# A twelve-part transformer step on one core: the dense network as one stage over chunks, and a retention that also norms and turns for the quantised network behind it

## The chip, the core and the metric

The kernel is one program on one core of a Trainium2 chip (eight cores, five engines each: PE or TensorE, DVE or VectorE, ACT or ScalarE, POOL or GpSimd, SP or SyncE). The metric is the device time of one execution in microseconds (us), lower is better; the time before is the median of 3 runs.

## What is computed

The input x has 128 rows of 32 positions with 128 channels, so 4096 tokens of 128 channels in float32. Twelve parts are added to it, each on a layer norm of the running x. Three are cross attentions over a context of 257 tokens, one is a linear transformer of six layers, three are mixtures of experts, and so on. Cut to what the change touches:

```python
x = x + _L2_attn_ref(_layernorm(x, axis=-1), ...)    # 8: retention
x = x + _L2_ffn_ref(_layernorm(x, axis=-1), L2_ffn_w1, L2_ffn_b1, L2_ffn_w2, L2_ffn_b2)   # 9: quantised network
...
x = x + _L3_attn_ref(_layernorm(x, axis=-1), ...)    # 11: its _block is below

def quant_act_uint8(x):
    s = jax.lax.stop_gradient(jnp.maximum(jnp.max(x), EPS)) / 255.0
    q = jnp.clip(jnp.round(x / s), 0.0, 255.0) * s
    return (_ste(x, q), s)

# inside _block of part 11, behind its attention
h2 = _layernorm(hs, ln2_g, ln2_b)
m = _student_linear(h2, *cf)        # 128 -> 512
m = _gelu_new(m)
m = _student_linear(m, *cm)         # 512 -> 128
return hs + m
```

The quantised network needs the largest value of its whole normed input before it can use any of it.

## The kernel before

`program` keeps the running x in SBUF as X, 32 tiles of 128 tokens by 128 channels, and runs the twelve parts one after the other. CHUNKS is 8 and TPC is 4: a chunk is four tiles, 512 tokens. A part is a `Scope` with tiles, semaphores and one block in which each engine has its own written-out list of instructions; engines meet only at semaphores. When a block closes, all engines meet, and POOL clears the scope's semaphores one after the other before the next block opens. `retention` has 33 semaphores and one for its weights, a `front` 15, `experts` 11.

**Retention** (part 8) is one pipeline over 32 tiles. Every engine runs `step(s)` for s from -16 to 41, and in a step each helper runs for the chunk whose place it is: `run(s, (4, squares))` runs `squares(c)` when s = 4c + 4. A tile's scores go from PE (`scores`, L965) to DVE (`decay`, L1116) and back to PE (`weighted`, L979). Each chunk is also normed by ACT (`apply`, L1052), turned by PE (`turn_normed`, L988), projected (L993, L1011, L1016), and afterwards centred and scaled by group (DVE L1125, L1129, L1134, L1140, ACT L1069, L1076, POOL L937), turned back (`turn_outputs`, L1022), gated (POOL L941), projected (`output`, L1029) and added to X (`add`, DVE L1145, place 9). The gate's Silu (ACT L1065) and the square root (ACT L1076) each have an ACT_TABLE_LOAD ahead of them in every chunk.

**The front of the quantised network** is a scope of its own, `front(core, "q_front", lambda n: None, hT_all)`. It works in pairs of chunks: DVE takes statistics of X (L207, L211), POOL makes the reciprocal root (L223, L225), DVE applies it (L233), PE turns the tiles (L1212), ACT copies them to `hT_all` (L1235), the transposed normed x of all 4096 tokens. `quantised_ffn` then fetches its weights with one DMA (SP, L151) and takes the maximum over hT_all on DVE (L2496).

**The dense network** of part 11 is two scopes: `front(core, "t_front", ...)` as above, here on the tile `inner` (written by the attention ahead of it, and the `hs` of the reference), and `experts(core, "t_mlp", source, hT_all, None, 1, 4, "gelu_tanh", base=inner, out_bias=True)`. `experts` is a hardware loop (`Fori`) over the eight chunks on each engine, here with one job of four blocks:

```python
last = pe.matmul(psum[:, (m % RING) * width + half], w("up")[...], rhs, ...)      # L1798, x4
act.wait_ge(s_base, c + 1)                                                        # before the first gelu
act.activation(hidden[:, j % 2, f], psum[:, at], ACT.Gelu_apprx_tanh, ...)        # L1851, x4
last = pe.matmul(psum[:, 4 + j % 2, ...], hidden[:, j % 2, f, ...], w("down")[...], ...)   # L1810, x16
dve.tensor_tensor(X[:, chunk], X[:, chunk], spread(w("bo"), TPC, 1), ALU.add)     # L1863
dve.tensor_tensor(X[:, chunk], X[:, chunk], base[:, chunk], ALU.add)              # L1866, counts s_base
dve.tensor_tensor(X[:, chunk], psum[:, 4 + j % 2]..., X[:, chunk], ALU.add)       # L1883
dve.wait_ge(s_acc, c * NJ + NJ)                                                   # end of the chunk
```

The order on PE is up(c), down(c), up(c+1), and so on. A float32 matmul is two records in the profile, so one chunk shows 8 of L1798 and 32 of L1810; a transposition of a tile is one record.

## Time and profile before

| what | us |
|---|---|
| median of 3 runs | 4488.55 |
| lowest and highest run | 4482.6, 4489.98 |
| the profiled execution, its own time | 4482.12 |
| its span | 4480.1 |
| mean granted TensorE clock, share of full speed | 0.893 |

The profile shows one execution. A row of the timeline has the start in us from the span's start, the time from the first start to the last end of the merged instructions, the engine, the line, the operation with output and inputs, the count, and in brackets the idle time of the engine just before and who ended it. PEld is the weight load of PE; PEq or ACTq is a sequencer. PEclk is the clock granted to TensorE as a share of 2.4 GHz, so 0.50 is 1.2 GHz.

### The profile page before, as it was taken

To read this page: it belongs to the slowest core of one execution; us is meant where nothing else is said; L and a number is where in the kernel's file an instruction comes from. 1 tells how busy PE (TensorE), PEld (TensorE's weight loads), DVE (VectorE), ACT (ScalarE), POOL (GpSimd) and SP (SyncE) were. 2 spreads that over 40 slices of the span, in tenths; PEclk is the share of its full clock that TensorE was granted. 3 is DMA by queue.
4 is the path that set the end of the run, shared out by engine and by line. 5 is a ranking of instruction groups with operands and counts; after the bars stand their busy time and mean duration, and the time that the engine had idled before them with its cause. 6 is when DMAs were issued, how large, how long until landed. Compare 5 with 4: busy or idle time off the path is not lost. (4 is left out here: it accounts for less than half of the span.)

```text
span 4480.1 us, 120532 instructions
## 1 busy us (share of the span) xinstructions
PE 3517.0 (79%) x44658; PEld 2454.9 (55%) x44662; DVE 2798.7 (62%) x7126; ACT 2349.8 (52%) x5817; POOL 2433.9 (54%) x2753
## 2 busy tenths in 40 slices
PE   7999779999997289793885999975399995866736
PEld 5666556666665166462663666643166664443424
DVE  6888756666665423574344888845678886734635
ACT  6777545555554044581223777732377774634613
POOL 6666566666664433673335666642166664805633
PEclk9999989999999599895997999986599998977958
DMA  2111100000000122101221111000011111000023
GB/s 65 35 35 35 66 17 10 5 7 10 10 2 7 53 75 66 39 5 53 74 62 45 35 35 35 30 7 7 14 32 35 34 35 49 3 1 6 3 77 89
DMA packets 90220, 145.81 MB, mean 33 GB/s; under 512 B 9984, under 2 KB 66432, under 8 KB 89344
## 3 DMA queue, kind: packets, MB, share of 16 engines
q1 hardware_dynamic: 79616, 119.72, 8.4%
q0 software_dynamic: 10240, 20.99, 1.5%
q8 instruction: 258, 4.23, 0.4%
q14 instruction: 106, 0.87, 0.1%
HBM read 109.61 MB, written 31.06 MB: 31 GB/s over the span
## 5 line engine op out<-in xcount | busy, mean ns | idle before, releaser
L2036 POOL TENSOR_TENSOR t_cross_E<-t_cross_E,t_cross_inverse 128x1028 f32<-128x1028 f32 x128 | 243.4, 1902 | 167.7 <-DVE t_cross_inverse L2308 167.7
L2036 POOL TENSOR_TENSOR e_cross_E<-e_cross_E,e_cross_inverse 128x1028 f32<-128x1028 f32 x128 | 243.3, 1901 | 162.1 <-DVE e_cross_inverse L2308 162.1
L2036 POOL TENSOR_TENSOR a_cross_E<-a_cross_E,a_cross_inverse 128x1028 f32<-128x1028 f32 x128 | 243.3, 1901 | 158.2 <-DVE a_cross_inverse L2308 158.2
L2894 PE MATMUL l_psum<-l_ffn_w,l_hidden 128*128 128x128 f32 x1536 | 218.0, 285 | 30.8 <-POOL l_hidden L2768 30.7
L2894 PEld LDWEIGHTS l_psum<-l_ffn_w,l_hidden 128*128 128x128 f32 x1536 | 190.6, 192 | 68.3 <-POOL l_hidden L2768 41.9
L2887 PE MATMUL l_psum<-l_hT,l_ffn_w 128*128 128x512 f32 x384 | 202.8, 631 | 1.0 <-ACT l_hT L2951 0.9
L2296 DVE TENSOR_REDUCE t_cross_negtop<-t_cross_psum 128x2 f32<-128x514 f32 x256 | 165.4, 688 | 51.6 <-PE t_cross_psum L2110 49.7
L2296 DVE TENSOR_REDUCE e_cross_negtop<-e_cross_psum 128x2 f32<-128x514 f32 x256 | 165.1, 686 | 43.9 <-PE e_cross_psum L2105 43.3
L2296 DVE TENSOR_REDUCE a_cross_negtop<-a_cross_psum 128x2 f32<-128x514 f32 x256 | 165.1, 686 | 42.3 <-PE a_cross_psum L2105 41.7
L2768 POOL TENSOR_TENSOR l_hidden<-l_hidden,l_less 128x512 f32<-128x512 f32 x96 | 120.0, 1272 | 92.1 <-ACT l_hidden L2975 92.1
L2747 POOL TENSOR_SCALAR l_normed<-inner,l_moments,l_rstd 128x128 f32<-128x128 f32 x192 | 160.4, 847 | 14.8 <-POOL l_rstd L2741 14.8
L3048 DVE TENSOR_TENSOR inner<-l_psum,inner 128x512 f32<-128x512 f32 x48 | 33.2, 691 | 212.9 <-PE l_psum L2879 212.9
L2758 POOL TENSOR_TENSOR l_q<-l_q,l_q_stat 128x512 f32<-128x512 f32 x48 | 50.9, 1060 | 182.6 <-DVE l_q_stat L3028 182.6
L2163 PE MATMUL e_cross_psum<-const_sb,e_cross_E 128*128 128x128 f32 x1024 | 133.7, 274 | 2.2 <-POOL e_cross_E L2036 2.1
L2163 PE MATMUL a_cross_psum<-const_sb,a_cross_E 128*128 128x128 f32 x1024 | 133.5, 274 | 2.2 <-POOL a_cross_E L2036 2.1
L2163 PE MATMUL t_cross_psum<-const_sb,t_cross_E 128*128 128x128 f32 x1024 | 133.2, 273 | 2.1 <-POOL t_cross_E L2036 2.1
L2871 PEld LDWEIGHTS l_psum<-l_qT,l_ctx 32*32 32x32 f32 x6144 | 65.5, 107 | 115.5 <-issue 109.8
L2231 ACT ACTIVATE t_cross_kT<-t_cross_psum,t_cross_weights 128x257 f32<-128x257 f32 x128 | 61.0, 477 | 128.5 <-PE t_cross_psum L2089 128.5
L2231 ACT ACTIVATE e_cross_kT<-e_cross_psum,e_cross_weights 128x257 f32<-128x257 f32 x128 | 61.0, 477 | 122.4 <-PE e_cross_psum L2089 122.4
L2231 ACT ACTIVATE a_cross_kT<-a_cross_psum,a_cross_weights 128x257 f32<-128x257 f32 x128 | 61.0, 477 | 120.3 <-PE a_cross_psum L2089 120.3
L2248 ACT ACTIVATE t_cross_E<-t_cross_psum,t_cross_negtop 128x257 f32<-128x257 f32 x256 | 118.6, 473 | 1.0 <-DVE t_cross_negtop L2296 0.9
L2248 ACT ACTIVATE a_cross_E<-a_cross_psum,a_cross_negtop 128x257 f32<-128x257 f32 x256 | 118.6, 473 | 0.9 <-DVE a_cross_negtop L2296 0.9
(756 smaller groups left out, 11724.1 us busy)
## 6 DMA issues: line engine op xcount, KB each, us to landing
a_cross_context<-context SPq DMA_DIRECT2D x32, 546.0 KB, 3.5
e_cross_context<-context SPq DMA_DIRECT2D x32, 546.0 KB, 3.5
t_cross_context<-context SPq DMA_DIRECT2D x32, 546.0 KB, 3.5
u_moe_all_weights<-pack_u_moe SPq DMA_DIRECT2D x1, 5633.0 KB, 16.7
slots<-l_blank SPq DMA_DIRECT2D x6, 832.0 KB, 12.1
a_moe_x_slots<-slots SPq DMA_DIRECT2D x26, 192.0 KB, 3.0
slots<-a_moe_y_slots SPq DMA_DIRECT2D x26, 192.0 KB, 2.1
c_moe_x_slots<-slots SPq DMA_DIRECT2D x26, 192.0 KB, 2.9
```

What stands on the lines that cost most here:

```text
L2036: pool.tensor_tensor(E[:, n % N], E[:, n % N], spread(inverse[:, n % 4], SK, 2), ALU.mult).then_inc(s_unit, 1)
L2163: last = pe.transpose(psum[:, (T_BANK, K_BANK)[c], g * P:(g + 1) * P], E[:, n % N, g, c * P:(c + 1) * P], ident)
L2231: act.activation(kT[:, n % 2], psum[:, K_BANK, 0:SK], ACT.Identity, bias=w("bk")).then_inc(s_k, 1)
L2248: act.activation(E[:, n % N, g], psum[:, g, 0:SK], ACT.Exp, bias=negtop[:, n % 2, g:g + 1], accum_out=total[:, n % 2, g:g + 1]).then_inc(s ...
L2296: dve.tensor_reduce(negtop[:, n % 2, at], psum[:, at, 0:SK], AX.X, ALU.max, negate=True).then_inc(s_top, 1)
L2747: last = pool.tensor_scalar(Y1[:, t], c.tile(t), moments[:, 0, t, 0:1], rstd[:, 0, 1, t:t + 1], ALU.subtract, ALU.mult)
L2758: pool.tensor_tensor(groups, groups, spread(q_stat[:, 2], DH, 2), ALU.mult).then_inc(s_soft, 1)
L2768: pool.tensor_tensor(hidden[:, f], hidden[:, f], less[:, f - 2], ALU.add).then_inc(s_late, 1)
L2871: last = pe.matmul(psum[rows, C_BANK, b * S:(b + 1) * S], ctx[rows, b], qT[rows, b * S:(b + 1) * S], start=True, stop=True)
L2887: pe.matmul(psum[:, U_BANKS[f % 2]], c.ffn(f * P), hT2[:], start=True, stop=True).then_inc(s_up, 1)
L2894: last = pe.matmul(psum[:, D_BANK, t * P:(t + 1) * P], hidden[:, f, t * P:(t + 1) * P], c.ffn((NF + f) * P), start=(f == 0 and t == 0), st ...
L3048: dve.tensor_tensor(c.chunk(), tiles(psum[:, C_BANK]), c.chunk(), ALU.add).then_inc(s_mid, 1)
```

## The change

Retention takes `hT_all` and does the next part's norm itself. Six helpers are added, each once per chunk: on DVE `statistics2` (place 9, behind the add) and `aggregate2` (place 10), on POOL `deviation2` (place 10), on ACT `apply2` (place 12) and `next_out` (place 14), on PE `turn_next` (place 14). The steps go on to s = 46, eight semaphores are added, and `q_front` is gone. `experts` and `t_front` are replaced by `mlp`, one scope of 13 semaphores written out for all eight chunks without a hardware loop; the bias and `inner` are added to X by POOL.

```diff
-def retention(core, name, weights):
+def retention(core, name, weights, hT_all):
...
+            def deviation2(c):
+                if c > 0:
+                    pool.wait_ge(s_norm2, TPC * c)
+                pool.wait_ge(s_moments2, c + 1)
+                pool.tensor_tensor(rstd2[:], moments2[:, :, 1], core.const("eps5"), ALU.add).then_inc(s_var2, 1)
...
+                pool.tensor_tensor(rstd2[:], rstd2[:], core.const("mhalf"), ALU.pow).then_inc(s_rstd2, 1)
...
+                pool.tensor_tensor(shift2[:], moments2[:, :, 0], rstd2[:], ALU.mult).then_inc(s_shift2, 1)
...
+                pool.tensor_tensor(shift2[:], core.const("zero"), shift2[:], ALU.subtract).then_inc(s_shift2, 1)
...
+                    if c >= 4:
+                        pe.wait_ge(s_hT2, c - 3)
...
+            def turn_next(c):
+                pe.wait_ge(s_norm2, TPC * c + TPC)
+                if c + 2 < CHUNKS:
+                    pe.wait_ge(s_centred, c + 3)
+                for t in range(TPC):
+                    last = pe.transpose(psum[:, O_BANK + c % 2, t * P:(t + 1) * P], Y2[:, t], ident)
+                last.then_inc(s_turn2, 1)
...
-                run(s, (-5, turn_normed), (-4, swapped_keys), (-3, swapped_queries), (-2, gates), (8, output))
+                run(s, (-5, turn_normed), (-4, swapped_keys), (-3, swapped_queries), (-2, gates), (8, output), (14, turn_next))
...
+            def apply2(c):
+                act.wait_ge(s_shift2, 2 * c + 2)
+                if c > 0:
+                    act.wait_ge(s_turn2, c)
+                for t in range(TPC):
+                    act.activation(Y2[:, t], X[:, c * TPC + t], ACT.Identity, bias=shift2[:, t:t + 1],
+                                   scale=rstd2[:, t:t + 1]).then_inc(s_norm2, 1)
+
+            def next_out(c):
+                act.wait_ge(s_turn2, c + 1)
+                act.activation(hT_all[:, c * CHUNK:(c + 1) * CHUNK], psum[:, O_BANK + c % 2], ACT.Copy).then_inc(s_hT2, 1)
...
-                run(s, (-5, normed_out), (-2, gates_out), (4, squares), (5, roots))
+                run(s, (-5, normed_out), (-2, gates_out), (4, squares), (5, roots), (12, apply2), (14, next_out))
...
+            def statistics2(c):
+                dve.wait_ge(s_done, c + 1)
+                for t in range(TPC):
+                    last = dve.bn_stats(stats2[:, t], X[:, c * TPC + t])
...
-                run(s, (4, centre), (-4, lambda c: term(c, 1)), (-3, lambda c: term(c, 3)))
+                run(s, (4, centre), (-4, lambda c: term(c, 1)), (-3, lambda c: term(c, 3)), (9, statistics2), (10, aggregate2))
...
-            front(core, "q_front", lambda n: None, hT_all)
             quantised_ffn(core, "q_ffn", "q_ffn", hT_all)
...
-            front(core, "t_front", source, hT_all, second=("eps5", False), keep=(inner, "source"))
-            experts(core, "t_mlp", source, hT_all, None, 1, 4, "gelu_tanh", base=inner, out_bias=True)
+            mlp(core, "t_mlp", source, inner)
```

The core of `mlp`, engine by engine (in the changed file):

```python
# POOL
deviation(0)
deviation(1)
for c in range(CHUNKS):
    if c + 2 < CHUNKS:
        deviation(c + 2)
    residual(c)          # X += bo, X += inner, one tensor_tensor over 128x512 each
# PE
turn(0)
for c in range(CHUNKS + 1):
    if c < CHUNKS:
        up(c)            # waits s_hT, and block by block s_hidden of chunk c - 1
    if c + 1 < CHUNKS:
        turn(c + 1)      # waits s_norm
    if c > 0:
        down(c - 1)      # waits s_hidden, and s_done of chunk c - 3
# ACT
normed_out(0)
for c in range(CHUNKS):
    activate(c)          # four gelus
    if c + 1 < CHUNKS:
        normed_out(c + 1)
# DVE
statistics(0)
statistics(1)
apply(0)
for c in range(CHUNKS + 1):
    if c + 1 < CHUNKS:
        apply(c + 1)     # four tensor_scalar
    if c + 2 < CHUNKS:
        statistics(c + 2)
    if c > 0:
        add(c - 1)       # waits s_down and s_base
```

How the change moves instructions. PE in retention around s = 26, before:

```order
L1011 MATMUL retention_psum<-retention_weights,retention_hT 128x128 x4
L979 MATMUL retention_psum<-retention_v_tok,retention_decayed 32x16 x32
L1016 MATMUL retention_psum<-retention_hT,retention_weights 128x512
L965 MATMUL retention_psum<-retention_q_heads,retention_kT 32x64 x16
L1022 MATMUL retention_psum<-const_sb,retention_centred 128x128 x4
```

and with the change:

```order
L1033 MATMUL retention_psum<-retention_weights,retention_hT 128x128 x4
L1001 MATMUL retention_psum<-retention_v_tok,retention_decayed 32x16 x32
L1038 MATMUL retention_psum<-retention_hT,retention_weights 128x512
L1059 MATMUL retention_psum<-const_sb,retention_normed2 128x128 x4
L985 MATMUL retention_psum<-retention_q_heads,retention_kT 32x64 x16
L1044 MATMUL retention_psum<-const_sb,retention_centred 128x128 x4
```

Four transpositions of the next part's normed tiles (L1059) stand between the gate's projection and the next tile's scores.

ACT in retention over one chunk, before (the two table loads are not in this view):

```order
L1069 ACTIVATE retention_square<-retention_centred 128x512
L1052 ACTIVATE retention_normed<-X,retention_shift,retention_rstd 128x128
L1076 ACTIVATE retention_group_root<-retention_group_var,const_sb 128x32
L1061 ACTIVATE retention_v_tok<-retention_psum 128x512
L1052 ACTIVATE retention_normed<-X,retention_shift,retention_rstd 128x128
L1065 ACTIVATE retention_gate<-retention_psum 128x512
L1080 ACTIVATE retention_aT<-retention_psum,retention_weights 128x512
```

and with the change:

```order
L1099 ACTIVATE retention_square<-retention_centred 128x512
L1117 ACTIVATE retention_normed2<-X,retention_shift2,retention_rstd2 128x128 x4
L1082 ACTIVATE retention_normed<-X,retention_shift,retention_rstd 128x128
L1106 ACTIVATE retention_group_root<-retention_group_var,const_sb 128x32
L1091 ACTIVATE retention_v_tok<-retention_psum 128x512
L1082 ACTIVATE retention_normed<-X,retention_shift,retention_rstd 128x128
L1095 ACTIVATE retention_gate<-retention_psum 128x512
L1122 ACTIVATE hT_all<-retention_psum 128x512
L1110 ACTIVATE retention_aT<-retention_psum,retention_weights 128x512
```

The four applies (L1117) stand between squares and roots, the copy to hT_all (L1122) between the gate and the output's copy.

PE in the dense network, before (two scopes, the second a loop over eight chunks):

```order
L1212 MATMUL t_front_psum<-const_sb,t_front_normed2 128x128 x32
...
L1798 MATMUL t_mlp_psum<-hT_all,generated 128x512 x4
...
L1810 MATMUL t_mlp_psum<-generated,t_mlp_hidden 128x128 x16
```

and with the change, up to the third chunk:

```order
L1858 MATMUL t_mlp_psum<-const_sb,t_mlp_normed 128x128 x4
L1866 MATMUL t_mlp_psum<-t_mlp_hT,generated 128x512 x4
L1858 MATMUL t_mlp_psum<-const_sb,t_mlp_normed 128x128 x4
L1866 MATMUL t_mlp_psum<-t_mlp_hT,generated 128x512 x4
L1858 MATMUL t_mlp_psum<-const_sb,t_mlp_normed 128x128 x4
L1874 MATMUL t_mlp_psum<-generated,t_mlp_hidden 128x128 x16
L1866 MATMUL t_mlp_psum<-t_mlp_hT,generated 128x512 x4
```

Between a chunk's up and its down PE now has the next chunk's up and the transpositions of the one after it.

## Rows read from the trace of the kernel before

**Rows 1.** The page's head: the span of the profiled execution.
```profile
span 4480.1 us, 120532 instructions
```

**Rows 2.** Windows: busy us of each engine in a stretch, then PEclk.
```profile
core 0: us, PE busy (x) PEld busy (x) DVE busy (x) ACT busy (x) POOL busy (x), PEclk, DMA share, GB/s
...
3935.95:4046.30 110.35, 70.05 (x352) 46.90 (x352) 35.09 (x121) 36.09 (x48) 9.65 (x16) 0.82 0.00 0
...
2979.32:2996.42 17.10, 15.65 (x420) 9.41 (x419) 8.13 (x21) 7.62 (x13) 8.78 (x13) 0.80 0.01 3
...
3024.92:3039.17 14.25, 12.67 (x420) 7.78 (x419) 7.09 (x13) 7.61 (x13) 7.16 (x9) 1.00 0.02 5
```

**Rows 3.** Timeline, from retention's last add through q_front to q_ffn's DMA.
```profile
3081.01 0.69 DVE L1145 TENSOR_TENSOR X<-retention_psum,X 128x512 f32<-128x512 f32 x1 [6.63 <-PE retention_psum L1029]
3084.46 0.88 DVE L207 BATCH_NORM_STATS2 q_front_ln_stats<-X 128x6 f32<-128x128 f32 x4 [2.75 <-PEq L165]
3085.48 0.38 DVE L211 BATCH_NORM_AGGREGATE q_front_ln_moments<-q_front_ln_stats 128x2 f32<-128x6 f32 x4
...
3087.27 1.11 DVE L233 TENSOR_SCALAR q_front_normed<-X,q_front_ln_moments,q_front_ln_rstd 128x128 f32<-128x128 f32 x4
...
3088.44 1.11 PE L1212 MATMUL q_front_psum<-const_sb,q_front_normed 128*128 128x128 f32 x4 [7.47 <-DVE q_front_normed L233]
...
3106.63 0.60 ACT L1235 ACTIVATE hT_all<-q_front_psum 128x512 f32<-128x512 f32 x1 [0.68 <-PE q_front_psum L1212]
3108.70 0.34 SPq L151 DMA_DIRECT2D q_ffn_weights<-pack_q_ffn  x1
```

**Rows 4.** Timeline: POOL's four small operations of a deviation, and four applies on ACT.
```profile
2942.91 0.20 POOL L911 TENSOR_TENSOR retention_rstd<-retention_moments,const_sb 128x4 f32<-128x4 f32 x1 [4.82 <-DVE retention_moments L1102]
...
2944.56 0.20 POOL L917 TENSOR_TENSOR retention_shift<-const_sb,retention_shift 128x4 f32<-128x4 f32 x1
...
4051.36 1.65 ACT L611 ACTIVATE inner<-X,u_self_shift,u_self_rstd 128x128 f32<-128x128 f32 x4 [9.79 <-POOL u_self_shift L358]
```

**Rows 5.** Timeline: one chunk in the middle of retention.
```profile
3035.46 0.32 ACT L1076 ACTIVATE retention_group_root<-retention_group_var,const_sb 128x32 f32<-128x32 f32 x1 [1.06 <-DVE retention_group_var L1134]
...
3036.99 0.34 DVE L1140 RECIPROCAL retention_group_rstd<-retention_group_root 128x32 f32<-128x32 f32 x1
...
3039.75 0.60 ACT L1065 ACTIVATE retention_gate<-retention_psum 128x512 f32<-128x512 f32 x1
...
3040.49 0.63 PE L1022 MATMUL retention_psum<-const_sb,retention_centred 128*128 128x128 f32 x4 [0.93 <-ACT retention_gate L1065]
...
3041.16 0.78 ACT L1080 ACTIVATE retention_aT<-retention_psum,retention_weights 128x512 f32<-128x512 f32 x1 [0.81 <-PE retention_psum L1022]
...
3041.71 0.66 PE L988 MATMUL retention_psum<-const_sb,retention_normed 128*128 128x128 f32 x4
...
3042.01 1.26 POOL L941 TENSOR_TENSOR retention_gated<-retention_aT,retention_gate 128x512 f32<-128x512 f32 x1 [1.65 <-ACT retention_aT L1080]
```

**Rows 6.** Timeline: squares and roots of retention's last chunk.
```profile
3071.80 0.63 ACT L1069 ACTIVATE retention_square<-retention_centred 128x512 f32<-128x512 f32 x1 [3.79 <-DVE retention_centred L1129]
...
3073.67 0.32 ACT L1076 ACTIVATE retention_group_root<-retention_group_var,const_sb 128x32 f32<-128x32 f32 x1 [1.25 <-DVE retention_group_var L1134]
```

**Rows 7.** Timeline of the dense network: t_front's first copy, then t_mlp.
```profile
3944.74 0.78 ACT L1235 ACTIVATE hT_all<-t_front_psum,generated 128x512 f32<-128x512 f32 x1 [11.63 <-PE t_front_psum L1212]
...
3970.84 6.38 PE L1798 MATMUL t_mlp_psum<-hT_all,generated 128*128 x8 [2.71 <-PEq L165]
...
3981.67 3.60 PE L1798 MATMUL t_mlp_psum<-hT_all,generated 128*128 x8
...
3984.66 2.42 ACT L1851 ACTIVATE t_mlp_hidden<-t_mlp_psum,generated 128x512 f32<-128x512 f32 x4 [0.58 <-DVE X L1866]
3987.13 3.84 PE L1810 MATMUL t_mlp_psum<-generated,t_mlp_hidden 128*128 128x128 f32 x32 [1.86 <-ACT t_mlp_hidden L1851]
...
4045.56 0.69 DVE L1883 TENSOR_TENSOR X<-t_mlp_psum,X 128x512 f32 x1 [6.46 <-PE t_mlp_psum L1810]
4047.66 0.34 SPq L151 DMA_DIRECT2D u_self_weights<-pack_u_self  x1
```

More of the change, by code:

```diff
@@ L946, in step @@
                     heads(s + 2)
-                run(s, (6, unit), (7, open_gate), (TPC - STATS, deviation))
+                run(s, (6, unit), (7, open_gate), (TPC - STATS, deviation), (10, deviation2))
             steps(step)
@@ L1747, in routed_experts, with mlp @@
         slots.s_put, slots.s_got = (s_put, puts + 16 * HALF * K), (s_got, gots + 16 * HALF * K // 2)
-def experts(core, name, weights, hT_all, comb, E, nf, kind, base=None, shared=False, out_bias=False, b2=False):
+def mlp(core, name, w, base):
     nc, X = core.nc, core.X
-    pair = kind in ("silu", "glu")
-    width = 2 if pair else 1
-    jobs = [(e, nf) for e in range(E)] + ([(E, 1)] if shared else [])
-    NJ = len(jobs)
-    blocks = sum(n for _, n in jobs)
-    first_block = [sum(n for _, n in jobs[:e]) for e in range(NJ)]
-    RING = 4 // width
+    F, T_BANK, D_BANK = 4, 6, 4
+    ident = core.const("ident")
@@ new lines, in mlp, with at @@
+        s_stats, s_moments, s_var, s_rstd = sc.sem("stats"), sc.sem("moments"), sc.sem("var"), sc.sem("rstd")
+        s_norm, s_turn, s_hT, s_up = sc.sem("norm"), sc.sem("turn"), sc.sem("hT"), sc.sem("up")
+        s_hidden, s_down, s_bias, s_base, s_done = (sc.sem("hidden"), sc.sem("down"), sc.sem("bias"), sc.sem("base"),
+                                                    sc.sem("done"))
+        block = sc.open_block()
+        def at(c):
+            return slice(c * TPC, (c + 1) * TPC)
+        @block.gpsimd
@@ new lines, in turn, with up @@
+            def turn(c):
+                pe.wait_ge(s_norm, c + 1)
+                if c > 0:
+                    pe.wait_ge(s_hT, c)
+                for k in range(TPC):
+                    last = pe.transpose(psum[:, T_BANK, k * P:(k + 1) * P], Y[:, c % 2, k], ident)
+                last.then_inc(s_turn, 1)
+            def up(c):
+                pe.wait_ge(s_hT, c + 1)
+                for f in range(F):
+                    if c > 0:
+                        pe.wait_ge(s_hidden, F * (c - 1) + f + 1)
+                    pe.matmul(psum[:, f], w("up")[:, f * P:(f + 1) * P], hT[:, c % 2], start=True, stop=True).then_inc(s_up, 1)
@@ new lines, in down @@
+            def down(c):
+                pe.wait_ge(s_hidden, F * c + F)
+                if c >= 2:
+                    pe.wait_ge(s_done, c - 1)
+                for k in range(TPC):
+                    for f in range(F):
+                        last = pe.matmul(psum[:, D_BANK + c % 2, k * P:(k + 1) * P], hidden[:, c % 2, f, k * P:(k + 1) * P],
+                                         w("down")[:, f * P:(f + 1) * P], start=(f == 0), stop=(f == F - 1))
+                last.then_inc(s_down, 1)
@@ new lines, in normed_out, with activate @@
+            def normed_out(c):
+                act.wait_ge(s_turn, c + 1)
+                if c >= 2:
+                    act.wait_ge(s_up, F * (c - 1))
+                act.activation(hT[:, c % 2], psum[:, T_BANK], ACT.Identity, bias=w("ln_b"), scale=w("ln_w")).then_inc(s_hT, 1)
+            def activate(c):
+                for f in range(F):
+                    act.wait_ge(s_up, F * c + f + 1)
+                    if f == 0 and c >= 2:
+                        act.wait_ge(s_down, c - 1)
+                    act.activation(hidden[:, c % 2, f], psum[:, f], ACT.Gelu_apprx_tanh, bias=w("b1")[:, f:f + 1]).then_inc(s_hidden, 1)
@@ new lines, in statistics, with apply @@
+            def statistics(c):
+                for k in range(TPC):
+                    last = dve.bn_stats(stats[:, c % 2, k], base[:, c * TPC + k])
+                last.then_inc(s_stats, 1)
+                if c >= 2:
+                    dve.wait_ge(s_norm, c - 1)
+                dve.wait_ge(s_stats, c + 1)
+                for k in range(TPC):
+                    last = dve.bn_aggr(moments[:, c % 2, k], stats[:, c % 2, k])
+                last.then_inc(s_moments, 1)
+            def apply(c):
+                dve.wait_ge(s_rstd, c + 1)
+                if c >= 2:
+                    dve.wait_ge(s_turn, c - 1)
+                for k in range(TPC):
+                    last = dve.tensor_scalar(Y[:, c % 2, k], base[:, c * TPC + k], moments[:, c % 2, k, 0:1], rstd[:, c % 2, k:k + 1],
+                                             ALU.subtract, ALU.mult)
+                last.then_inc(s_norm, 1)
@@ L1909, in experts @@
+            dve.wait_ge(s_done, CHUNKS)
         sc.close_block()
@@ L3184, in program @@
             4: lambda: self_attention(core, "c_self", r8, ("c_cross", "c_self"), (context32, None), (True, False)),
-            8: lambda: retention(core, "retention", "retention"),
+            8: lambda: retention(core, "retention", "retention", hT_all),
         }
```

168 lines of the change are left out of this document (41 added, 127 removed).

## The prediction

> **What bounds the kernel now.** The parts run one after the other with a meeting of all engines between them, so a stage is worth what its own chain takes, not what the engines' shares of the span say. I read the timeline around the two places the change touches, then the windows over them; the chain that ended last on the page covers only the last part and says nothing here. The profiled execution has a span of 4480.1 us [rows 1] and a time of 4482.12, so 2.0 lie around the span. It is 6.4 under the median of 4488.55; I work in its microseconds and move the difference over to the median.
>
> Place one is the seam between retention and the quantised network [rows 3]. Retention's last add ends at 3081.70, the front's first statistics start at 3084.46, its last copy ends at 3107.23, and SP issues the next weights at 3108.70. The 27.0 us between 3081.70 and 3108.70 are two meetings of 2.8 and 1.5 and 22.8 of a front that every engine mostly waits in. Place two is the dense network with its front, 110.4 us from 3935.95 to 4046.30, in which PE is busy for 70.05 at a granted clock of 0.82 [rows 2]. Its loop is serial [rows 7]: the second chunk's down starts at 3987.13; the eighth starts 3.94 ahead of the add at 4045.56, at 4041.62; six periods, 9.08 each. In a period PE idles 1.86 for the last gelu, and DVE idles 6.46 for PE. The first gelu at 3984.66 was held not by PE but by DVE's two additions into X, which stand behind the last chunk's add. So up, which is through at 3985.3, hides nothing of the gelus.
>
> **The dense network, step by step.** Up to ACT's first copy at 3944.74 [rows 7] the new stage does what the old front does, so it starts there. The copy ends at 3945.52 and up(0) starts at 3945.6. Its eight records took 6.38 before, mostly at 1.2 GHz, since TensorE had been nearly idle [rows 7]; it has been nearly idle here too, so I take 6.4, to 3952.0. Up(1) must wait for the last gelu and then the copy of hT: a quarter of 2.42 rounded up to 0.7, 0.78, and two hand-offs of 0.1, so 3953.7. From there PE has work all the time: seven ups at 3.44 (the eight records of 3.60 less the tail of the last, 3.01/7 = 0.43 each), six transpositions at 0.58 to 0.66 [rows 5], eight downs at 3.65 (3.84 less its last record's tail). That is 24.1 + 3.5 + 29.2 = 56.8, to 4010.5, and with 0.2 of tail and an add of 0.69 to 4011.4. The old end is 4046.25, so 34.8 are saved. Two semaphores more than `experts` cost 0.1 in the clearing. **Term one: 34.7.**
>
> What must hide under PE's 7.6 us per chunk: ACT has four gelus and a copy, 2.42 + 0.78 = 3.2; DVE has statistics 0.88, aggregation 0.38, four applies 1.11 [rows 3] and an add 0.69, 3.2 with gaps; POOL has two small operations of 1.3 together and two additions over 128x512. The nearest row for such an addition is POOL's 1.26 [rows 5], so 3.9. The tightest deadline is DVE's: behind down(c-1) it adds and applies chunk c+1, 0.1 + 0.69 + 1.15, while PE's next up takes 3.44. It has 1.5 to spare. Should the activation table be reloaded between gelus and copy, that would fall on an ACT that has 4.4 free.
>
> **Retention, step by step.** In the loop [rows 2]: a chunk takes 14.25, in which PE is busy 12.67, DVE 7.09, ACT 7.61, POOL 7.16. Each chunk gets about 0.6 on PE, 1.3 on DVE, 1.65 + 0.60 on ACT, 1.85 on POOL [rows 3, 4]. No engine is filled, so only the places matter. I take them one by one with [rows 5]. The transpositions stand ahead of scores and of `turn_outputs`, which idles 0.93 for ACT's gate at 3040.35; 0.6 fits into that. The gate waits for its table load, not for PE, so it doesn't move. The copy to hT_all then runs from 3040.35 to 3040.95 and ACT's next copy starts at 3041.16. The four applies push the roots from 3035.46 to about 3036.4; DVE uses them at 3036.99, but has its statistics of 0.88 ahead of that and comes 0.9 later itself, to 3038.3. POOL's scaling of 512 columns, at most the 1.26 of its gating, then ends at 3039.6, and `turn_outputs` wants it at 3040.49. POOL's deviation, 1.85, and one tile's heads (half the columns, so 0.63) bring it to 3042.2, and the gating at 3042.01 slips by 0.2, into slack. In the loop I take **0**. The bounds are 0 less a gain (below) and, if ACT's applies and copy go on the path, 2.0 a chunk.
>
> At the end the cover is thin. The applies of chunk 5 stand behind the squares of the last chunk, which end at 3072.43; the roots at 3073.67 move to 3074.4, **0.7** [rows 6]. One set of transpositions at the low clock, 1.11 less its last record's tail [rows 3], stands between two tiles' scores: **0.8** at most. So the last add ends near 3083.2. Behind it comes the one chunk of norm that nothing hides: statistics and aggregation 1.45 with their gap [rows 3], POOL's four 1.93 from hand-off on, ACT's four applies 1.75 [rows 4], PE's turn 1.16, ACT's copy 0.72 [rows 3]: 7.0, to 3090.2. The meeting behind retention took 2.76 for 34 semaphores and the one behind the dense network 1.41 for 11 [rows 3, 7], which makes 0.06 each, so eight more give 3.25. SP then issues at 3093.5, not at 3108.70. **Term two: 15.2.**
>
> **The sum.** 34.7 + 15.2 = 49.9, so 4432.2 for the profiled execution and **4438.7** for the median. What is measured here can tell some 0.2%, 9 us.
>
> **A rule against a row.** In the chunk from 2979.32 the granted clock is 0.80 and the chunk takes 17.10, not 14.25 [rows 2]: the clock fell to 1.2 GHz in it, costing 2.85, though PE had been busy for most of the chunk. Since the row gives no sign which way the change pushes this, I leave the 2.85 in, as a bound on both sides. The Trainium skill ("TensorE: Matmul & The Clock Gate", "The HAM clock gate") says that throttled is the default and that activity releases it, and that the moment of release differs from run to run. By that rule the transpositions, which fill an idle wait of PE, would keep the clock up and give 2.85 back, 4435.8; by the row alone it is 4438.7. The trace agrees with the rule's first half where PE had little to do: up(0) behind the old front ran at 1.2 GHz, 6.38 against 3.60 [rows 7].
>
> **Rivals.**
> - *The added work shows in retention's loop.* For: the slacks I count on are 0.2 to 0.9 us, and ACT's queue is in order. Against: PE idles 0.93 just behind the new transpositions. At 2.0 a chunk, 16 in all: 4455. Chance 0.10.
> - *DVE and POOL get in each other's way in the dense network.* POOL's two additions are long (1.26 each), and no row shows one beside a DVE tensor_scalar with both operands in SBUF. If each holds DVE up once between down and the next turn, DVE's 1.94 becomes 4.5, 1.05 past the 3.44 it has, so 1.05 six times, 6.3: 4445. Against: POOL starts its additions 1.3 behind the statistics and is through before the next down ends, by 0.3. Chance 0.12. The Trainium skill ("SBUF — State Buffer", the shared port pair) states this as a rule: the pair is locked for a whole instruction and the loser blocks; by it this rival holds wherever the two meet; no row here shows it.
> - *The dense network doesn't do what its order says* and keeps its period of 9.08 through a wait that I miss (s_done, s_turn): 1.5 more for seven chunks, 10.5: 4449. Chance 0.05.
> - *Slower: PE gets stuck at turn_next.* It is in order, and the next tile's scores are behind it. If the chain from add to applies (5.1 of the 7.0) is late for it in every chunk, each chunk pays up to 7.0, 56 in all, and the clock falls in each, 2.85 more for eight, 23. Less the 49.9, that is 4518. It decides from 6.2 a chunk on. Against: place 14 is five steps, some 18 us, behind the add. Chance 0.03, a third of it for a loss just large enough to cancel the gain.
>
> **Chances and range.** Forecast as worked out 0.70. Faster 0.96, same 0.01, slower 0.03. On the low side the forecast's bounds are 2.85 for the clock, 1.5 for the end of retention, 3 for an earlier rise of the clock under up(0) (half of its 6.4), and 4 for the scatter of the median (the lowest run lies 6 under it): 4427. On the high side the range takes in the first three rivals: 4456.
>
> **What would show it.** In the profile after: no gap of 23 us ahead of the SP issue behind retention, and 10 to 12 us from retention's last add to it; chunks of retention still 14.25 apart; roots 0.9 later but the same start of `turn_outputs` within 0.2. In the dense network: PE idle once, 1.7 us behind up(0), and then ups 7.6 apart at clock 1.00; the add waits for PE, never PE for DVE; 75 us from the first statistics to the last add. I would be wrong if PE's rows there showed waits for DVE's applies, if retention's chunks grew, or if the seam's chain ran well past 7.0.

## The result, and the profile after

| what | before | after |
|---|---|---|
| median, 4 runs each on the same chip | 4485.58 | 4430.60 |
| lowest to highest | 4478.73 to 4489.98 | 4427.85 to 4435.16 |
| the profiled execution, time | 4482.12 | 4429.09 |
| its span | 4480.1 | 4427.2 |

The ratio is 0.988, with a 95% interval of 0.9863 to 0.9897, so the kernel gained 1.2%, clear of the noise: 55.0 us in the medians, 53.0 in the two profiled executions. The forecast was 49.9 less. The page's head of the changed kernel, for [rows 1]:

```profile
span 4427.2 us, 120386 instructions
```

Windows of the changed kernel, for [rows 2]: an interval between two `turn_outputs` early in retention, one later, and the dense network from its first statistics to its last add (the stretch, its length, each engine's busy time, PEclk).

```profile
core 0: us, PE busy (x) PEld busy (x) DVE busy (x) ACT busy (x) POOL busy (x), PEclk, DMA share, GB/s
2984.76:2999.06 14.30, 12.71 (x418) 7.78 (x419) 8.99 (x29) 7.61 (x12) 8.83 (x13) 1.00 0.01 3
3013.32:3027.57 14.25, 13.10 (x422) 8.27 (x423) 8.36 (x25) 9.64 (x18) 10.31 (x17) 1.00 0.01 3
3924.46:3995.19 70.73, 62.79 (x352) 44.89 (x352) 28.46 (x104) 28.85 (x41) 29.81 (x32) 0.93 0.00 1
```

The second window holds all that was added to a chunk: ACT and POOL work 2.0 and 1.5 more than in the same interval before (7.62 and 8.77), and the interval is 14.25 long as ever. From its first statistics to its last add the dense network took 106.75 before, at a clock of 0.83, and takes 70.73 at 0.93. (The 110.35 of [rows 2] starts at the end of t_self's last add, 3.55 ahead of the first statistics; counted so, the changed kernel takes 74.16.) The window before:

```profile
3939.50:4046.25 106.75, 70.05 (x352) 46.90 (x352) 35.08 (x120) 36.09 (x48) 9.65 (x16) 0.83 0.00 0
```

The seam behind retention, timeline, for [rows 3]:

```profile
3081.70 0.69 DVE L1187 TENSOR_TENSOR X<-retention_psum,X 128x512 f32<-128x512 f32 x1 [6.40 <-PE retention_psum L1051]
3082.43 0.87 DVE L1192 BATCH_NORM_STATS2 retention_stats<-X 128x6 f32<-128x128 f32 x4
...
3083.86 0.20 POOL L931 TENSOR_TENSOR retention_rstd<-retention_moments,const_sb 128x4 f32<-128x4 f32 x1 [4.32 <-DVE retention_moments L1200]
...
3085.75 1.65 ACT L1117 ACTIVATE retention_normed<-X,retention_shift,retention_rstd 128x128 f32<-128x128 f32 x4 [2.59 <-POOL retention_shift L937]
...
3087.44 1.12 PE L1059 MATMUL retention_psum<-const_sb,retention_normed 128*128 128x128 f32 x4 [4.92 <-ACT retention_normed L1117]
3088.60 0.60 ACT L1122 ACTIVATE hT_all<-retention_psum 128x512 f32<-128x512 f32 x1 [1.21 <-PE retention_psum L1059]
3092.40 0.34 SPq L151 DMA_DIRECT2D q_ffn_weights<-pack_q_ffn  x1
```

From the end of the last add, 3082.39, the chain of norm and turn takes 6.8 to 3089.20 (7.0 forecast), the closing 3.20 (3.25 forecast). The seam is 10.0 instead of 27.0.

One chunk in retention, for [rows 5]. `turn_next` (L1059) stands ahead of the scores and of `turn_outputs` (L1044), whose wait for ACT's gate is 0.49 where it was 0.93:

```profile
3041.82 0.63 PE L1044 MATMUL retention_psum<-const_sb,retention_centred 128*128 128x128 f32 x4 [0.49 <-ACT retention_gate L1095]
```

The end of the dense network, for [rows 7]. The ups (L1866) start at 3930.32, 3937.27, and then 7.45 apart (the first time 7.55) up to 3974.60; between the last two are 9.12:

```profile
3930.32 5.50 PE L1866 MATMUL t_mlp_psum<-t_mlp_hT,generated 128*128 128x512 f32 x8 [0.87 <-ACT t_mlp_hT L1893]
...
3974.32 1.27 POOL L1840 TENSOR_TENSOR X<-X,generated 128x512 f32<-128x512 f32 x1
3974.60 3.60 PE L1866 MATMUL t_mlp_psum<-t_mlp_hT,generated 128*128 128x512 f32 x8
3974.80 0.69 DVE L1933 TENSOR_TENSOR X<-t_mlp_psum,X 128x512 f32<-128x512 f32 x1 [4.47 <-PE t_mlp_psum L1874]
3975.41 4.19 DVE L1926 TENSOR_SCALAR t_mlp_normed<-inner,t_mlp_moments,t_mlp_rstd 128x128 f32<-128x128 f32 x4
3975.67 1.27 POOL L1842 TENSOR_TENSOR X<-X,inner 128x512 f32<-128x512 f32 x1
3976.89 1.28 POOL L1840 TENSOR_TENSOR X<-X,generated 128x512 f32<-128x512 f32 x1
3978.25 1.26 POOL L1842 TENSOR_TENSOR X<-X,inner 128x512 f32<-128x512 f32 x1
3979.65 0.66 PE L1858 MATMUL t_mlp_psum<-const_sb,t_mlp_normed 128*128 128x128 f32 x4 [1.46 <-DVE t_mlp_normed L1926]
...
3983.72 3.60 PE L1866 MATMUL t_mlp_psum<-t_mlp_hT,generated 128*128 128x512 f32 x8
...
3994.50 0.69 DVE L1933 TENSOR_TENSOR X<-t_mlp_psum,X 128x512 f32<-128x512 f32 x1 [2.88 <-PE t_mlp_psum L1874]
3996.77 0.34 SPq L151 DMA_DIRECT2D u_self_weights<-pack_u_self  x1
```

PE waits once for DVE's four applies, which take 4.19 instead of 1.11, while POOL has two residuals (four additions) back to back. In the six periods ahead of it PE doesn't wait for the applies.

**Where the time went, by the two traces.** From t_self's last add to SP's issue behind the dense network: 111.71 before, 75.74 now, 36.0 saved (forecast 34.7). From retention's first key product to SP's issue behind it: 168.76 before (from 2939.94), 147.69 now (from 2944.71), 21.1 saved (forecast 15.2). Together 57.0; the untouched rest of the program was 4.1 longer in this pair. That lies in one mixture of experts ahead of retention, 375.7 before and 380.6 after between two of SP's issues; in the profiles of the first set below it took 373.2 to 375.7, in those of the other two 379.7 to 380.9, whatever the kernel. The surplus of 5.9 over the forecast of 15.2 is, but for 0.25 of the seam, in retention itself: it should have become 1.5 longer at its end, and from first key product to last add it went from 141.76 to 137.68. Of these 4.1 less, 2.8 are the first interval between two `turn_outputs`, which was 17.09 and is 14.30; 0.7 lie ahead of the first `turn_outputs` and 0.6 between the sixth and the last.

### The profile page after: what moved, and what is told of

Same layout as the page of the kernel before. It is cut to its first block and busy times, and to the rows that moved or that the text cites. A ratio compares the mean times of both kernels' runs of the same rounds, so it can differ in the third digit from the quotient of the medians.

```text
span 4427.2 us, 120386 instructions
## 1 busy us (share of the span) xinstructions
PE 3505.0 (79%) x44658; PEld 2449.9 (55%) x44662; DVE 2783.6 (63%) x7078; ACT 2354.7 (53%) x5842; POOL 2457.0 (55%) x2785
```

## The experiments

Ratios are against the kernel before on the same chip, with their 95% intervals. "Retention's length" is from its first key product to the end of its last add; the "intervals" are the first five between its `turn_outputs`. An interval is 14.25 (the fifth 13.87) or, at a clock of 0.80, 17.1 (16.7). Each run has one profiled execution, so a length or an interval is that of one execution, while a ratio goes over all of them. "Old retention" is that of the kernel before, "new" that of the change.

### First set: the two halves, and both kernels again

**Dense network alone.** The kernel before, with this edit:

```diff
-            front(core, "t_front", source, hT_all, second=("eps5", False), keep=(inner, "source"))
-            experts(core, "t_mlp", source, hT_all, None, 1, 4, "gelu_tanh", base=inner, out_bias=True)
+            mlp(core, "t_mlp", source, inner)
```

> Half of the change: the dense network as one stage, retention and the quantised network's front as before. The prediction's term one gives 34.7 us less than before; the profile after, between the last add of t_self and SP's issue for the last layer, gives 36.0. If the two halves don't touch each other, 34.7 to 37. If part of this gain was only scatter of other parts: under 33. The one collision of DVE's applies with POOL's additions ahead of the last up (about 1.5 us, an up 9.1 behind the one before instead of 7.45) should be there again if POOL's order makes it; if it was chance it is gone.

Measured: ratio 0.991 (0.9893 to 0.9927), so 32.7 to 47.9 less than 4479.81, which holds the 34.7 to 37 expected. The last up is 9.13 behind the one before, its applies in POOL's way again.

**Retention alone.** The changed kernel, with the old front and `experts` for the dense network.

> The other half: retention norms and turns for the quantised network, dense network in two stages as before. Term two gives 15.2. In the profile after, from retention's first key product to SP's issue behind it, 21.1 were saved, since retention itself took 137.7 instead of 141.8. Theory A (the transpositions and copies fill PE's waits and keep its clock up, a steady gain): 19 to 21 less than before, retention 137 to 138 long with no chunk at a clock of 0.80. Theory B (the clock's fall in one chunk and PE's small issue gaps come and go by chance, with or without the change): about 16 on the median, and retention's length differs between profiles of the same code by 3 us or so.

Measured: ratio 0.9955 (0.9938 to 0.9973), 20.2 less, of an interval of 12.1 to 27.8. Retention's length 140.52, with one interval of 17.10 (the second), which Theory A had ruled out. The interval of the gain holds both theories' figures.

**The kernel before again.** No edit.

> The kernel before, once more, for the scatter of its untouched parts. Theory A: retention takes 141 to 142 from first key product to last add again, with one chunk of 17.1 at a clock of 0.80. Theory B: the fall sits in another chunk or is missing, and the length lies anywhere between 138 and 142. Ratio to before 1.000 within 0.2%.

Measured: ratio 0.9999 (0.9984 to 1.0013). Retention's length is 149.22, outside what either theory allowed, with four intervals of 17.1 in a row, and it is 150.45 with four in the dense-only kernel, whose retention is the old one. Windows of this run, interval by interval:

```profile
2973.47:2987.72 14.25, 12.68 (x419) 7.79 (x419) 7.93 (x21) 7.61 (x12) 8.77 (x12) 1.00 0.01 3
2987.72:3004.82 17.10, 15.65 (x419) 9.42 (x419) 8.13 (x21) 7.61 (x12) 8.76 (x12) 0.80 0.02 4
3004.82:3021.91 17.09, 15.75 (x418) 9.48 (x419) 7.28 (x14) 7.61 (x12) 8.76 (x12) 0.80 0.01 3
3021.91:3039.01 17.10, 15.65 (x419) 9.42 (x419) 7.19 (x13) 7.61 (x12) 7.14 (x8) 0.80 0.01 3
3039.01:3055.72 16.71, 15.64 (x418) 9.41 (x419) 7.13 (x13) 6.08 (x8) 6.89 (x8) 0.80 0.01 3
```

And pieces of the third of them. The clock is not lowered by a fifth throughout: it is at its lower level (0.50, 1.2 GHz) for some 7 us and at 1.00 (2.4 GHz) for the rest, at the same place in each interval, from some 2.5 behind the start of `turn_outputs` on:

```profile
3007.50:3013.50 6.00, 6.00 (x74) 3.42 (x75) 2.97 (x6) 1.74 (x4) 2.55 (x7) 0.50 0.01 3
3014.50:3019.00 4.50, 4.37 (x134) 2.54 (x138) 3.27 (x7) 0.44 (x2) 1.34 (x3) 1.00 0.02 4
```

**The changed kernel again.** No edit.

> The changed kernel, once more. Theory A: retention takes 137 to 138, all chunks 14.25 but the first. Theory B: a fall of the clock turns up in some chunk and makes it 140 or more. Time 49.9 (the prediction) to 57 (the sum of the two places in the profile after) under before; the sum of the two halves' gains if they are independent. Ahead of retention the profile after was 4.8 us longer than before in code that is the same; that should not come back.

Measured: ratio 0.9875 (0.9856 to 0.9894), 56.0 less, of 47.5 to 64.5. Retention's length 137.89, no slow interval. The two halves' gains add up to it (0.9 and 0.45 per cent against 1.25, within the intervals).

What follows: the 2.85 that the prediction saw in one interval is a state that comes and often stays in the old retention, 1, 4 and 4 of five intervals in three profiles, and seldom in the new one, 0, 1 and 0. Neither theory as written fits: B is right that the length of the old code differs between profiles, by 8.7 rather than 3 or 4, A that the new code is steadier.

### Second set: what holds the clock, the collision, and the rival on the other side

**Idle transpositions alone.** The kernel before, with this in PE's list:

```diff
+            def fill(c):
+                if c + 2 < CHUNKS:
+                    pe.wait_ge(s_centred, c + 3)
+                    for t in range(TPC):
+                        pe.transpose(psum[:, O_BANK + c % 2, t * P:(t + 1) * P], w("wq"), ident)
-                run(s, ..., (8, output))
+                run(s, ..., (8, output), (14, fill))
```

> The kernel before, with nothing but six sets of four transpositions of a weight tile into the free output bank, in PE's queue at the place where the change puts turn_next (chunks 0 to 5; nobody reads them). In six profiles so far, the second to fifth interval between turn_outputs was 17.1 at a clock of 0.80 in 9 of 12 intervals of the old retention (1, 4 and 4 of four) and in 1 of 12 of the new. Theory A (PE's work in that place keeps its clock up): at most 1 of 4 slow here, retention 138 to 141 from first key product to last add, time 3 to 10 under before. Theory B (something else of the change, or chance): 3 or 4 of 4 slow, 147 to 150, ratio 1.000. Theory C (the work costs its own length): 0.6 more for each of six.

(The 9 of 12 is a slip: the one slow interval of the first profile is its first, so it was 8 of 12 for the second to fifth, and among all first five 9 of 15 for the old retention and 1 of 15 for the new.) Measured: ratio 0.9973 (0.9962 to 0.9984), 12.1 less, of 7.2 to 17.1. More PE work, and a faster kernel. The profile: 17.13, 17.10, 14.26, 14.25, 13.87; length 142.17. One of the second to fifth is slow, as Theory A allows; the length is over its 138 to 141, since the first interval is slow too. The second interval is the last one that starts ahead of the first `fill`:

```profile
3001.56:3018.66 17.10, 16.09 (x422) 9.92 (x423) 7.75 (x19) 7.62 (x12) 8.77 (x12) 0.80 0.02 4
3018.66:3032.92 14.26, 13.11 (x423) 8.29 (x423) 7.36 (x17) 7.62 (x12) 8.79 (x12) 1.00 0.01 3
```

Theory C falls: the four transpositions take PE 0.44 and the interval keeps its 14.25. Three intervals behind the first `fill` can give back 8.6 at most (three times 2.85), which lies in the interval of the timing; what the rest of the 12.1 is, if it is more than scatter, no profile shows.

**One transposition instead of four.** The changed kernel with `for t in range(TPC if c + 2 >= CHUNKS else 1)` in `turn_next`.

> The changed kernel with one transposition instead of four in turn_next for chunks 0 to 5 (three quarters of those chunks' turned rows are left out); norm, applies and copies stay. Theory A, if it takes PE's work: the 17.1 intervals come back, 2 to 4 of four, retention 143 to 150, time 6 to 10 over the changed kernel's. Theory B, if the other engines' work or shifted starts did it: 0 or 1 of four, 138, time as the changed kernel (0.9875 of before).

Measured: ratio 0.9853 (0.9838 to 0.9868); intervals 14.28, 17.08, 14.25, 14.25, 13.87; length 141.13. It is as fast as the two kernels with four that were timed on the same chip (0.9857 and 0.986, below), and the intervals behind the first `turn_next` are all fast. So PE's full added work isn't what it takes: a single transposition (0.14) in that place, together with the rest of the change, was enough in this profile. Whether the rest of the change would do it without any transposition was not tried: no kernel here has all of it and leaves them out.

**POOL's additions kept off DVE's applies.** The changed kernel with

```diff
             def residual(c):
+                if c + 2 >= CHUNKS:
+                    pool.wait_ge(s_norm, CHUNKS)
```

> The changed kernel, with POOL's residual of chunks 6 and 7 held until DVE has applied chunk 7 (one wait on s_norm). Theory P (DVE's applies of both operands in SBUF are held by POOL's additions): the applies ahead of the last up take 1.1 instead of 4.2, PE doesn't wait for them, the last up comes 7.45 behind the one before instead of 9.1, 1.6 less in the stage (65.7 to 64.1 from first copy to last add). Rival (the four applies were long for their own reasons, such as the data or the moments just written): they stay at 3 to 4 and nothing is saved. By the median this is under what can be told, so the trace decides.

Measured, timeline of the same place: the applies take 1.11 again, POOL's additions stand behind them, and the last up follows after 7.44.

```profile
3977.84 3.60 PE L1868 MATMUL t_mlp_psum<-t_mlp_hT,generated 128*128 128x512 f32 x8
...
3978.64 1.11 DVE L1928 TENSOR_SCALAR t_mlp_normed<-inner,t_mlp_moments,t_mlp_rstd 128x128 f32<-128x128 f32 x4
3979.83 1.27 POOL L1842 TENSOR_TENSOR X<-X,generated 128x512 f32<-128x512 f32 x1 [2.23 <-DVE t_mlp_normed L1928]
...
3985.28 3.60 PE L1868 MATMUL t_mlp_psum<-t_mlp_hT,generated 128*128 128x512 f32 x8
```

From the first copy (3932.70) to the last add's end (3996.75) are 64.05, 1.65 less than 65.70. The collision is shown, cause and cure: the six other profiles of the new dense network without this wait have 9.12 or 9.13 between the last two ups, the three that are built on this one have 7.45. The ratio, 0.9857 (0.9842 to 0.9872), can't resolve it.

**turn_next too early.** The changed kernel with `(12, turn_next)`, `(11, apply2)`, `(12, next_out)`.

> The changed kernel with turn_next and its copy at place 12 instead of 14, the applies at 11: the slower rival of the prediction (PE stuck at turn_next) made on purpose. PE then waits in its queue for the centring of chunk c+2, which DVE does in the same step: sums and centring 1.4 with hand-offs 1.7, minus what PE has anyway. Expected: PE waits for DVE's centring ahead of turn_next in each of the first six chunks, 1 to 2.5 each, intervals between turn_outputs 15.5 to 17 instead of 14.25, 8 to 15 us over the changed kernel, ratio to before 0.990 to 0.992. If the queue has slack there: no difference.

Measured: ratio 0.986 (0.9845 to 0.9875). Intervals 17.10, 17.64, 14.69, 14.69, 14.30; length 145.41. PE doesn't wait for the centring, which is done by then. But at place 12 no wait covers the transpositions, and `turn_outputs` waits for ACT's gate for its full 0.93 again:

```profile
3027.24 0.60 PE L1059 MATMUL retention_psum<-const_sb,retention_normed 128*128 128x128 f32 x4
...
3035.61 0.30 PE L1044 MATMUL retention_psum<-const_sb,retention_centred 128*128 128x128 f32 x1 [0.93 <-ACT retention_gate L1095]
```

So a chunk costs 0.44 more, the transpositions' own length. The expectation had the price two to five times too high, and the wrong mechanism. The three intervals behind the first `turn_next` are at a clock of 1.00 all the same, though the idle of 0.93 is there: filling that one idle is not the condition.

### Third set: a semaphore's price, and further gains

**40 unused semaphores** in retention's scope.

> The changed kernel with 40 semaphores more in retention's scope, which nothing uses but the clearing behind it. The prediction priced a semaphore at 0.06 from two meetings (34 and 11 semaphores, 2.76 and 1.41). Expected: from the last copy into hT_all to SP's issue 3.2 + 2.4 = 5.6 instead of 3.20. If the difference of those two meetings had another reason: 3.2 to 4.

Measured: the last copy ends at 3095.84, SP issues at 3101.61, 5.77 instead of 3.20, so 0.064 for each semaphore. (The ratio, 0.9869, has the interval 0.985 to 0.9889.)

**Weights and maxima early.** On top of the kept-off additions: the last layer's weights are allocated outside both scopes and fetched in retention's block, and

```diff
+            def peak(c):
+                dve.wait_ge(s_hT2, c + 1)
+                dve.tensor_reduce(peaks[:, c:c + 1], hT_all[:, c * CHUNK:(c + 1) * CHUNK], AX.X, ALU.max)
-            link(dve.tensor_reduce(peak[:, 0:1], hT_all[:], AX.X, ALU.max))
+            link(dve.tensor_reduce(peak[:, 0:1], peaks, AX.X, ALU.max))
```

> A further step on the seam, on top of e2_port: the last layer's weights are fetched during retention, and DVE takes the maximum of each chunk of hT_all in retention, so that 4.42 of reduction over 4096 columns becomes one over 8. In the profile after, the reduction started 3.8 behind SP's issue, for the weights. Expected: 3.8 for the transfer and 4.2 for the reduction saved, less 0.8 for the last chunk's maximum behind the last copy: 7.2, and no more in retention's loop than its one DVE operation of 0.7 a chunk, which is hidden; ratio to before 0.984 to 0.986. If DVE's added operation shows in the loop: 0.7 a chunk, and only 2 are left of the gain.

Measured: from retention's last add to the first operation on the weights 10.96 (3084.72 to 3095.68); in the profile after it was 18.26 (3082.39 to 3100.65, both edges from its timeline). That is 7.3 less, against 7.2 expected. Intervals 15.55, 14.25, 14.26, 14.25, 13.87: DVE's added 0.7 is hidden. Ratio 0.9863 (0.9847 to 0.9879), which can't be told from 0.9857 of the kernel it builds on.

**Transpositions in the first two intervals as well.** `fill` as above at steps 6 and 10, ahead of the first two `turn_outputs`.

> e2_more, with four transpositions of a weight tile into the free output bank ahead of each of the first two turn_outputs, where turn_next has none yet. In ten profiles so far the intervals that start with a turn_outputs that has transpositions in the step before it never fell to 0.80 (0 of 21), those without did in 16 of 29. Theory A (PE's added work in that place holds the clock): 0 of 5 intervals slow, retention at 137 to 138 from first key product to last add; 2 to 3 less than e2_more on the average. Rival (the third interval on is safe for another reason): a slow interval turns up among the first two, as in 7 of 14 so far.

Measured: all five intervals at a clock of 1.00 (14.26, 14.26, 14.26, 14.34, 13.87), length 137.67; the first two:

```profile
2988.75:3003.01 14.26, 13.11 (x422) 8.29 (x423) 8.99 (x30) 7.62 (x12) 8.82 (x13) 1.00 0.01 3
3003.01:3017.27 14.26, 13.11 (x422) 8.29 (x423) 8.69 (x29) 9.29 (x17) 10.29 (x17) 1.00 0.02 5
```

Ratio 0.9855 (0.9837 to 0.9873); the median is 2.3 under that of the kernel it builds on, which the intervals can't resolve. So the trace bears Theory A out, the timing doesn't decide it, and one profile with two fast intervals at its start is weak by itself: of the 24 first and second intervals without transpositions 12 were fast.

**Transpositions in the slow tail and ahead of the first up.**

> e3_guard, with idle transpositions in PE's waits at two places more where the granted clock is low: the last 20 us of retention (3, 7, 5 and 15 ahead of the last turn_outputs, output and turn_nexts), and the start of the dense network (11 ahead of the first turn, 3 behind it). Expected if work in the waits raises the clock: the last matmuls of retention (2.08 and 1.12 at the low clock) take 1.16 and 0.6, some 3 less up to SP's issue; up(0) 3.7 instead of 5.5 to 6.5, 2 less. Together 5 less than e3_guard. Rival (the filled work delays what stands behind it and the clock stays low): no less, or 1 to 3 more.

Measured: ratio 0.9848 (0.9831 to 0.9865). All five intervals fast again. In retention's tail the clock stayed at 0.50 up to 3085.58 and the chain up to the last add kept its times (the last output 2.08); only the last turn was faster, 0.66 instead of 1.12, behind fifteen idle transpositions:

```profile
3085.37 1.91 PE L979 MATMUL retention_psum<-const_sb,retention_weights 128*128 128x128 f32 x15
...
3089.43 0.66 PE L1071 MATMUL retention_psum<-const_sb,retention_normed 128*128 128x128 f32 x4 [2.15 <-ACT retention_normed L1137]
```

It wasn't these fifteen that raised the clock: it rose while the first of them ran. By then PE had been busy for 4.0 us without a gap, with the last output (2.08), the five idle transpositions ahead of the next turn and that turn itself. PE alone, busy time and clock ahead of the rise and behind it:

```profile
3081.58:3085.58 4.00, 4.00 (x18) 0.50 0.00 0
3085.87:3087.28 1.41, 1.41 (x13) 1.00 0.00 0
```

In the dense network up(1) starts 6.19 behind up(0). Without the transpositions that distance was 6.61 to 8.04 in nine profiles, so 0.4 to 1.9 is gained there. Against e3_guard's profile the end of retention gives 0.46 (last add to last copy 6.34 instead of 6.80) and the dense network 0.4, so 0.9 of the 5 expected; the medians differ by 1.0, which the intervals can't resolve. The rival is right about the tail, though nothing was lost by the filling.

## Why the prediction was right

The forecast case held. By its steps:

- **Term one, 34.7.** Measured 36.0 in the profiled pair. From SP's issue ahead of part 11 to the one behind it, four profiles with the old network took 272.2 to 273.5 and the first three with the new one 237.0 to 239.0: 35 on the average. Up(0) with the bubble was 6.95 in the profile after and up to 8.04 in others (8.1 forecast), the period 7.45 (7.6 forecast; its own terms add up to 7.67): a set of transpositions costs PE 0.44, not 0.58, since its tail overlaps too, and a down 3.57, not 3.65. The collision took 1.67 of the gain away again. The forecast "75 us from the first statistics" was counted from t_self's last add, 3.55 earlier; so counted it is 74.16.
- **The rival "DVE and POOL get in each other's way"** had the right mechanism and the wrong count. I expected it in each of six periods if at all. It is on the path once, 1.67, since only the last two residuals have no deviation ahead of them to hold them back until DVE is through. The applies at 3932.29 were held too (3.15 instead of 1.11), which is not on the path. The Trainium skill ("SBUF — State Buffer", "SBUF: two separate sides") says that a DVE operation in a 2-port performance mode, or with two SBUF inputs, and a GpSimd operation share a pair of ports, that whichever starts first has it for its whole instruction, and that the other blocks. The trace agrees for the applies (4.19 instead of 1.11; which of the two cases they are, it doesn't show), and in the same window DVE's add of 0.69, whose first operand is in PSUM, is not held beside POOL's addition.
- **Term two, the loop at 0.** Right as an argument on places: 14.25 with all the added work, and the transpositions hidden in the idle ahead of `turn_outputs`, 0.93 to 0.49. The early kernel shows what that place is worth, 0.44 a chunk. The roots start 4.54 ahead of `turn_outputs`, where they started 5.03 ahead, so they are 0.5 later and not 0.9.
- **Term two, the seam.** Forecast 3081.70 to 3108.70 less a chain of 7.0 and a closing of 3.25; measured 6.8 and 3.20. A semaphore is 0.064 by itself, 0.06 forecast.
- **The end of retention, +1.5.** Partly. From the last chunk's squares [rows 6] to the last add's start were 9.21 and are 9.69 (3072.01 to 3081.70). The four profiles of the old retention have 9.20 to 9.22, the ten of the new one 9.50 to 9.92, so the applies and what else was added cost 0.3 to 0.7 there. The 0.8 for one set of transpositions doesn't show: the interval it falls into is not longer (11.62, was 11.72).
- **The step that was mis-sized:** "I leave the 2.85 in, as a bound on both sides." The forecast kept the fall of the clock in the time after, and took it for one interval. It wasn't one interval of 17.10 but a state that the old retention is in for 1, 4 or 4 of five intervals, and the change nearly ended it. From SP's issue ahead of retention to the one behind it, the three profiles of the old code without `fill` took 180.1, 188.8 and 187.4, the first three of the new one 159.1, 161.8 and 159.2: 25 less on the average, not 15.2. The one profiled execution I had was by luck the one with the fewest falls; it showed 2.85 where the other two lost 11.4. The timings show 55.0 (medians) and 56.0 (ratio, again) less against 49.9. So the 25 of three profiles a side is more than the timings bear out: with the 35 of the dense network it would make 60. That the total came within 5 or 6 of the forecast is in part luck, since retention gave more than its term for a reason that the sum didn't hold. The rule that I had set beside the row, the Trainium skill's ("TensorE: Matmul & The Clock Gate", "The HAM clock gate"), that activity releases the throttle, would have pointed the right way.

**How sure the clock part is.** In all fourteen profiles, intervals whose start has transpositions added a step or a few ahead (from the third `turn_outputs` on in the changed family and in the kernel with `fill`, from the first on in the last two kernels) number 37, and none fell. The others number 33, and 18 fell, one of them only in part. That mixes places, so place by place: of the third to fifth intervals 6 of 9 fell without transpositions and 0 of 33 with them; of the first two, 12 of 24 without and 0 of 4 with them. Falls in one profile aren't independent of each other (the 6 are two profiles of three), but the place where they stop is the same each time, and the kernel with nothing but `fill` is faster by its timing alone. That transpositions in that place keep the old retention's clock up is shown by that kernel; that they, and not its other added work, do it in the changed kernel is argued from it. What stays open is what exactly the chip's clock answers to. It isn't the idle of 0.93, which the early kernel keeps, nor a large amount of work, since a single transposition of 0.14, with the rest of the change, was enough in the one profile that has it; and PE's busy share doesn't separate them either, since it lies between 89 and 94% in slow and fast intervals alike.

## What to carry to other kernels

Before pricing a serial loop's speed, look at the granted clock piece by piece and in more than one profile: a loop in which PE is busy 89% of the time can still fall into a state in which it loses 2.85 us of every 17.1, and a few idle transpositions in its waits were worth 7 to 17 us of 4496 here. Added work is hidden by its place in the queue, not by the engine's share: the same four transpositions cost nothing ahead of a wait and their whole length two steps earlier. Where POOL and DVE both work from SBUF, look for the iterations at the end of a loop in which POOL has lost whatever paced it.

## What was not expected of the hardware

- TensorE's granted clock fell to 1.2 GHz for some 7 us and then rose again, in up to four intervals in a row of a steady loop in which no idle of PE is longer than 0.93 us.
- In retention's last 18 us the clock is at 0.50. Between the last `turn_outputs` and the last add PE is busy for 3.2 of 5.4 us; filling its waits with transpositions (to 4.7 of 5.45) did not raise the clock there. It rose behind 4.0 us of unbroken work, and the last turn then took 0.66 instead of 1.12.
- Four DVE applies of 0.28 each took 4.19 together beside four POOL additions of 1.27, while POOL's additions kept their length.
